# The order in which each engine takes the steps of its strands, written anew

## The reference

```python
x = x + 0.5 * _L0_ffn_ref(_layernorm(x), ...)    # squared ReLU with a sigmoid gate and a time shift
x = x + _L0_attn_ref(_layernorm(x), ...)         # gated linear recurrence, 32 states
x = x + 0.5 * _L0_ffn_ref(...)
x = x + 0.5 * _L1_ffn_ref(...)                   # top-1 router over 8 experts, capacity, one shared weight
x = x + _L1_attn_ref(_layernorm(x), ...)         # Mamba forward and backward, 256 channels x 16 states
x = x + 0.5 * _L1_ffn_ref(...)
x = x + 0.5 * _L2_ffn_ref(...)                   # 16 experts, two chosen, and a shared one
x = x + _L2_attn_ref(_layernorm(x), ...)         # causal attention, 16 heads of 8
x = x + 0.5 * _L2_ffn_ref(...)
x = x + 0.5 * _L3_ffn_ref(...)                   # 8 experts, two chosen
x = x + _L3_attn_ref(_layernorm(x), ...)         # attention with normed q and k, 16 heads of 8
x = x + 0.5 * _L3_ffn_ref(...)
```

## Time and profile before

| quantity | value |
|---|---|
| median of 3 runs | 2844.74 us (2841.48 to 2850.73) |
| profiled execution, its own time | 2852.38 us |
| its span, first to last instruction | 2850.6 us |
| mean granted clock of TensorE | 0.922 |
| PE, DVE, ACT, POOL busy | 2455.4, 2273.0, 1692.7, 1377.6 us |
| instructions in the span | 31759 |
| moved by DMA | 251.37 MB, mean 88 GB/s |

### The profile page before, as it was taken

One profiled execution on the slowest core, in us unless ns is written; L12 is line 12 of the kernel. 1 busy time (PEld: TensorE's weight loads), 2 busy tenths in 40 slices (PEclk: granted clock), 3 DMA queues, 4 the chain that ended last, 5 costly groups with the idle time before them and its releaser, 6 DMA issues. The chain is left out here.

```text
span 2850.6 us, 31759 instructions
## 1 busy us (share of the span) xinstructions
PE 2455.4 (86%) x8664; PEld 881.1 (31%) x8664; DVE 2273.0 (80%) x3833; ACT 1692.7 (59%) x2849; POOL 1377.6 (48%) x1295
## 2 busy tenths in 40 slices
...
GB/s 96 102 111 99 117 107 62 104 104 138 64 105 65 96 128 100 49 105 129 100 106 50 116 90 123 60 97 107 124 67 136 73 62 58 46 77 48 44 25 34
DMA packets 159395, 251.37 MB, mean 88 GB/s; under 512 B 20089, under 2 KB 58233, under 8 KB 158961
## 3 DMA queue, kind: packets, MB, share of 16 engines
...
## 5 line engine op out<-in xcount | busy, mean ns | idle before, releaser
L1411 DVE TENSOR_REDUCE nmx<-ps 128x1 f32<-128x512 f32 (+3 forms) x864 | 536.2, 662 | 80.2 <-PE ps L621 78.5
L1802 ACT ACTIVATE tN<-ps 128x512 f32<-128x512 f32 (+1 forms) x896 | 463.8, 565 | 156.5 <-PE ps L621 154.3
L621 PE MATMUL ps<-tN,strip 128*64 128x512 f32 (+3 forms) x2048 | 476.8, 556 | 0.8 <-DVE hN L1434 0.6
L1910 POOL TENSOR_TENSOR rb<-duf,bs 128x512 f32<-128x512 f32 x256 | 324.2, 1280 | 235.0 <-DVE ps L1473 127.1
L1910 POOL TENSOR_TENSOR rb<-dub,bs 128x512 f32<-128x512 f32 x256 | 323.2, 1274 | 162.4 <-DVE ps L1473 84.1
L1473 DVE TENSOR_TENSOR_SCAN ps<-ps,rb 128x512 f32<-128x512 f32 x304 | 365.4, 1218 | 30.5 <-ACT ps L1856 28.5
L621 PE MATMUL ps<-hF,W 128*128 128x512 f32 x592 | 345.1, 667 | 51.2 <-DVE tF L1328 25.3
L621 PE MATMUL ps<-Ks,Qs 128*128 128x512 bf16 (+3 forms) x1024 | 297.5, 358 | 68.2 <-DVE nmx L1411 57.9
L1919 POOL TENSOR_TENSOR rh<-rh,cs 128x512 f32<-128x512 f32 x208 | 265.4, 1287 | 170.3 <-DVE rh L1473 166.4
L621 PE MATMUL ps<-tF,W 128*128 128x512 f32 x528 | 288.4, 633 | 19.7 <-POOL tF L1936 16.2
L1929 POOL TENSOR_TENSOR tF<-tF,cr 128x512 f32<-128x512 f32 x128 | 163.9, 1282 | 270.4 <-DVE tF L1332 158.0
...
## 6 DMA issues: line engine op xcount, KB each, us to landing
cr<-shares SPq DMA_DIRECT2D x248, 256.0 KB, 3.5
bs<-rowsf SPq DMA_DIRECT2D x128, 256.0 KB, 3.7
cs<-rowsf SPq DMA_DIRECT2D x128, 256.0 KB, 3.4
bs<-rowsb SPq DMA_DIRECT2D x128, 256.0 KB, 3.7
cs<-rowsb SPq DMA_DIRECT2D x128, 256.0 KB, 3.4
...
```

The costliest lines, as they stand in the source:

```text
L621: return eng.matmul(o, l, r, start=start, stop=stop, skip_group_check=skip_group_check)
L1411: red(nmx[:, 4 * qt + 2 * (i // 4) + a, i % 4:i % 4 + k], o[:, 0:k * nk].rearrange("p (k c) -> p k c", k=k), AX.X, ALU.max, negate=True).t ...
L1802: act(tN[m % NP][:, a, 0:nq], PA[a][:, 0:nq], ACT.Exp).then_inc(s_ex, 1)
L1910: tt(rb[n % NBB][:, g, :], du[p][:, g, :], bs[n % NB][:, :], ALU.mult).then_inc(s_bp[g], 1)
```

## The change

Only the table `ORDER` is written anew, for all five engines. The diff holds nothing else. In the kernel's own terms the sequence in which each engine takes its strands is made anew with the array's spacings as traced; the strands, their steps, tiles and semaphore waits are those of before. The first and the last lines of each text (the diff's lines in between are of the same kind):

```diff
--- before.py
+++ after.py
     "sp": (
-        "M1S25M1S32M1S26M1S18F1S2F4S3F1S1F1S4F2S4M1S10P1S2P2S1P7S9M1S2X1S7F1S1F4S3F1S1F1S4F2S18F4S2F2S2F1S2F1S2F1S2M1S8P1S4"
...
-        "S5P4F9X1F8P1F1P5F1P4F9P1X1P1F8P4F5P2F2P1F1P1F2X1F1P1F3P1F5P4F1P4F9X1F9P10X1F2X1F9"
+        "M1S29M1S30M1S34M1S10F1S2F3S2F2S2F2S2F1S4M1S12P1S4P9S8M1X1S8F4S4F2S4F2S4F1S16F4S3F1S1F1S3F1S1F1S2F1S2M1S8P1S2P7F1P1"
...
+        "X1F7"
     ),
     "pe": (
-        "L22M1L1M1L1M2L3M1L1M2L2M1D1L2S1D1S1L1D1S1L2D1S1D1L1S1L1D1S1L1D1S1M1L1D1S1L1D1S1M1L1M1D1S1L1D1S1M1D1S1L1D1S1D1S1M1"
-        "D1S1D1S1M1D1S1M1D1S1L1D1S1D1S1M1L1M1D1S1L1D1M1S1D1S1D1M1S1D1L1D1M1L1M1D1S1D1L1S2M1L1D1S1L1D1S1M1D1S1D1L1S1D1L2M1S1"
...
-        "L1A2L1A2L1A2L3A16X2A2X2A2X2A2X2A2X2A2X2A2X2A2X2A1X14A1X2F1X3F1X6A1X2F1X1A1X1A1X2A2X2A2X2A2X2A2X2A2X2A2X2A2X2A2X2F1"
-        "X1A1X1A2X1A3F1A4F1A2F1A2F4A2F1A2F1A28F16"
+        "L22M1L1M1L1M2L3M1L1M2L2M1S1L1D1S1L1D1S2D1S1D2M1S1D1S1L1D1S1D1S1L1D1L1D1S1M1D1M1L1D1S1L1D1M1S1L1D1S2L1S1D1L1S1D1M1"
+        "L1M1D1L1S1M1D1L1S1D1S1L1D1S1M1L1M1D1S1L1D1M1S1D1S1D1M1S1D1L1S2L1M1D1M1L1D1S3D1M1L1S1D1L1S1D1S1D1L1M1D1S1L2D1S1M1S1"
...
+        "F1A6F1A1F2A3F3A2F1A1F1A1L1A2L1A3L1A2L1A2L1A1L1A2L1A2L1A2L1A2L2A14X2A2X2A2X2A2X2A2X2A2X2A2X2A2X2A2X2A1X11A1X2F1X1F1"
+        "X7A1X2A1X1A1X1F1X2A2X2A2X2A2X2A2X2A2X2A2X2A2X2A2X2F1X1A1X1A1X2A3X1A9F4A31F4A1F17"
     ),
     "dve": (
-        "L24M2L1M8L1M2L2D2S2D1S1D1L1S1L1D1L1S1L1D1S1M1D1S1D1S1M1D1S1D1L1S1D1S1D1S1M1D1S1D1S1M1L1D1S1D1S1M1D1M1S1M1D1S1L1M1"
-        "D1S1D1S1L2D1S1D1S1L2M1D1S1D1S1L1D1S1D1S1M1D1S1D1S1L3D1S1D1S1L2D1S1D1S1M1D2S2D1S1M1D1S1D1S1L1D1S1D1S1L1D1S1D1S1L1D1"
...
-        "X1F6X1F9L1F4L1A1F1X3A1X2A1X7F1X2F1X1F7X1F1X1F1X1F1X1F1X1F1X1F1X1F1X1F2X3F2X2F2X3F2X5F2X3F2X3F2X3F2X3F2X2F1X5F1X7F1"
-        "X2F1X1F1X1F4X1F16L3A1X28A1X2A1X13F1X2F2X2F3X2F4X2F3X2F3X2F3X2F3X13A1F1A2F39"
+        "L24M2L1M8L1M2L1S1L1S1D1S1D1S1M1D1S1D1S1M1L1S1D1S1D1M1S1D1S1D1L1D1S1D1S1M1D1S1D1S1L1D1S1D1S1M1D1S1D1S1L1D1S1D1M1S1"
+        "D1M1D1S1D1M1D1S1L1D1S1D1S1D1S1D1M1S1D1S1D1S1L1S1D1S1D1M1S1D1S1D1S2D2L1M1D1S1L2D1M1S1L1D1L1S1L2D1L1D1L1S1L1S1L1D1L1"
...
+        "A1F1X3A1X2A1X7F1X2F1X1F14X1F2X3F2X3F2X3F2X6F2X3F2X3F2X3F2X3F2X3F1X5F1X7F1X2F1X1F1X1F1X1F1X1F1X1F1X1F5X1F11L3A1X27"
+        "A1X2A1X14F1X2F1X2F4X2F5X2F3X2F3X2F4X2F1X13A3F40"
     ),
     "act": (
-        "L30M2L2M3L2M2L2M1L1M2L2M8L2D1L2S1M2L2D1S1M1L2D1S1D1S1L2D1S1L2D1S1L2D1S1M1L1D1S1M1L1D1S1L3M1D1S1M1D1S1M4D1S1L2M3D1"
...
-        "L1A1L1A1L1A2L1A1L1A1L1A1L2A1L2A1L1A2L1A1L1A32F3A4F1A16F1A48F5"
+        "L30M2L2M3L2M2L2M1L1M2L2M8L2S1D1L1M2L2S1L1M1D1S1L2S1D1S1D1M1S1D2S1M1D1S1D1S1D1S1D1L2S1M1D1L2D1S1M2D1S1M2L1M1L1D1S1"
...
+        "F1A14F1A48F5"
     ),
     "pool": (
-        "L1M1D1S1D1S2D2S1D1S1L1D1S1D1S1D1S1D1S1L1D1S1D1S1D1S1D1S1D1S1D1S1M1D1S1D1S1D1S1D1S1M1D1S1D1S1D1S1D1S1D1S1D1S1D1S1D2"
...
-        "C2F3M1F5A2F3A1F5A5F9A1F1A1F2A1F1A1F3A3F2A1F7A1F3A1F2A1F2A5F14A1F2A10F5A1F3A2"
+        "L1M1S1D1S2D1S1D2S1D1S1D1S1D1S1D1S1D1S1D1S1L1D1S1D1S1D2S1D1S1D1S1L1M1S2D1S1D3M1S1D1S1D1S1D1S1D1S1D1S1D1S1D1S2D1S1D1"
...
+        "A10F3A1F3A2F2"
     ),
```

More of the change, by code:

```diff
@@ L69 @@
[L69 to L72, removed]
@@ new lines @@
+        "F1L1F1L1F1L1F2L3F1M1F2M1F3M1F1M1F2M1F2M1F4M1F4M1F1M1F4M1F3L1F1L1F1L1F1L6M2F1M1F1X2M1X3M1X2F1X2F1X1F1X5F1X4F1X1F1X3"
+        "F1X4F1X3L1X2F1L1X3F1X2L1X4L1X3F1L1F1L1X1F1L1A1L1A1L1A3L1A2L1F1A1M1A3F1A2F1A2M1A2F1A2F1M1A2M1A3M1A1F2L1A2F2L1F2A2F1"
+        "L1A2L1F1A1L1F1A1F1A2F1A2F1L1A2F1A1L1A1F1A2F2A2L1A1F1A2F1L1F1X1L1X1F1X2F1X4A1F1X2L1X1F1X3F1X2L1X3F2L1X3F1X3L1F1X3L1"
+        "F1X3L1X3F1X2F1X3L1X3L1X6F1L1X1F2X1F1L1X3F2L1X2F1X4L1X4M1X1F2M1F1X1F2M1F1M1A1F2A2F1A2M1A2F2A2M1F1A2F1A2F1A2F1A2M1A2"
@@ new lines @@
+        "F1A2F1A2F1A2F1A2M1A2F1A2F1M1A2F1A1M1F1A6L1A3L1A6F1L1A2L1F1A1L1A3L1A2L1F1L1A2L1A1F1A1M1A2F1A1M1F4X2F1A1X1M1A1X2M1F1"
+        "X2M1F1X6F1X1L1X3L1X4L1X3L1X4L1X2L1F1L1X1F1X4L1X2L1X3L1X2L1X1F1M1F2X1F3M1X1F2A1F1A2F1M1A2F2A1M1A4F1A2M1A2F1A2F1A1F1"
+        "L1A3F2L1A5L1A1L1F1A2F2L1A1F1A2F2L1F1A2F2A1L1F1A3F2A3F1L1A1F1A2F1L1A1F1L1A2F1A2F2L1X2A1F2X2F1L1X2F1X1L1X2F2X2F1X3F1"
+        "X3L1X2F1L1X3F1X2L1X5F2X1L1X5L1X5L1X2F1X1L1X3F1X1F1L1X2F1X2L1X1F1X1F1X1M1X2F1X1M1X3F2X4F1M1F1M1X1F2M1F1A1F1A2M1F1A2"
@@ new lines @@
+        "F1A2F1A2F1A2M1A2F1A2F1A2F1A2F1A2M1A1F1A1F1A2M1A1F1A1F1A2F1A2M1A2F1L2F1A2L1A2L1A2L1A2L1A2L1A2L1A2L1A2F1A2M1A2F1A2M1"
+        "A4F1A1F1A3M1F1A1F3M1A1F2X1M1F1X2F1X2L1F1X2L1X5L1X4L1X4L1X2L1X2L1F1X3F1L1X3L1X3L1X2L1X2M1F2X1F1X4F1X1F1X1F1M1F2X1F2"
+        "M1A1F2M1A2F1A1M1A2F1A3F1L1A1F1A2L1A2F1A2F1L1A3L1A2L1A2F1A2F2L1F1A2F2L1F1A2F1A2L1F2A2L2F2A2F1A2L1F2A3F1A3F1A2L1F1A1"
+        "F1A2L1X1F1X1F1X1A1F1X1L1X2F1L1X3F2X3L1X1F1X1F1X1L1X2F1L1X3F1X9F1X3F1X2L1X6L1X2F1L1X2F1X1F1X1L1X2F1X2M1F1X2F1X3F1X3"
@@ new lines @@
+        "L1X3L1X1F1X2F1X3L1F1X1F1X1M1F1X2F1X1M1X1F1X2F1X2F1X2M1X1F1M1F1M1X1F3M1F2A1F2A2F1A2M1F2A2F1A2F1A2M1A2M1A2F1A2F1A2F1"
+        "A2M1A2F1A2F1A2L1A2F1A2L1A2F1L1A1L1A5L1A2L1A2L1A2L1A2L1A2F1A2F1A2M1A4M1A2F1A2F1A2F1A1X2F1X2F1X1F1A1X2F2M1X3F1X2F1X1"
+        "M1X3M1F1X11L1X3L1X5F1X3F1X2L1X4L2X1F2L1F1L1A1F1A2F1A2L1A2F1A4F1A2F1A2F1A2F1A2L1A2F2A2L1A2L1F1M1A3F1A3F1A4F1A2M1A4"
+        "F1A2F1A4M1A1X2M1X4A1X1F1X3F1X2F1X2F1X3F1X2F1X2F1X3F1X1F1X3F1X3F1X2F1X2F1X14F1X3F1X2F1X3M1X1F1X2F1X3F1X1F3X1F2M1F1"
@@ new lines @@
+        "A1F1M1A2F1A5F1A1F1M1A2F2A2L1A4L1A6F1A2F2A2F1A2F2A2L1F1A2L1F2L1F1A2F2A2L1F1A2L1F2A2F1A2L1A2F1A2F1A2F1A2L1A2F1A2F1A2"
+        "F1A2M1F2A2F2A3M1F1X2F2A1X2F1M1X3M1X4M1X4F1X2F1X10F1X1F1X1F1X5F1X2F1X1F1X4F1X1F1X2L1F1X1L1F1L1A1F1L1A2L1A1F1L1F1L1"
+        "A3L1A2L1A1F1A1F1L1F1L1A2F2A2F1A2F2A2F1A4F1A2F2A4F1A2F1A4F1A2F1A4F1A2F1A2F1A2F1A1X2F1X1F1X2F1A1X1F1X1F2X3F1X5F1X2F1"
+        "X3F2X2F1X3F2X2F1X3F2X2F1X3F3X1F1X2F1X2F1X3F1X3L1F1X2L1F1X5L1F1L1F1L1F1X3L1X3L1X1L1X1F1L1X3F3X1F3A1F1A10F1A2F1A2F3"
@@ new lines @@
+        "D1M1X7M1X2M1X1M1X10D1X7F1X5S1D1X2L1X7F1X3F1X1F1X1F1S1F1S1F1D1X1F1S1F2D1F1S1L1F1D1F1S1D1L1S1D1S1D1S1D1S1F1D1F1M1D1"
+        "M1S1M1D1S1M1D1S1D1S1M1F1M1S1M1D1F1S1M1F1S1F1S1F1S1F2D1F2D1F1D1F1D1F1S1F2M1F2S1F2D1S2F1M1A1D1S1F1D2F1D1S1F1L1S1F1D1"
+        "S3D1S1F1L1D1S1D1F1D1S2D1F1S1D1S1D2F1D1S1D1S3F1L2F1S1D3F1D1S3F1X2S1X1L1X3A1L1F1A1X2L1F1X2D1X1L1X5F1X3F1D1X3L1F1X3D1"
+        "S1X3D1S1X3F1X2F1X1F1L1F1X1F1X1F2X1F2X1F1X1F1X1F1X1F1X1F1X1F1X1F1X1F2X1L1X2F1D1X1L1S1L1D1L1F1L1D1X1F1X2L1X1L1F1L2X1"
@@ new lines @@
+        "D1F1M1F1D1S1D1M1S3D1S1D1S1F1M2F1M1F1D1F1S1F1M1F4S1F1D1F1X1F1X1F1X1F1X1F1A1F1X1F2A1X2F1X4F1X3F1X4F1X3F1X4F1X3F1X4F1"
+        "X14F1X3M1D1F1X5F1X6F1X3F1X1M1X1D1F1X1F1X1D1S2F1S1M1F1D1S1D2M1F1S5D1F1D1S1F4D1F2S1F2D1F1D1F1S1F1S1F2D1F1D1F1S1F2D1"
+        "S1F1L1D1S1F1D1S2F1D2S1D1F1S1D1F1D1S1D1S1D1S1F1A1F1D1S1D1F1D1S2F1S2F1S1D2F1S1D1S2D1F1D1S2F1D1S1D2F1D2S1D1F1D1S2F1D1"
+        "S1D1F1M1D1S1D1S1D1F1M1A1S1X1S1X1A1F1X2F11X1F1M1F1X1F1X1F2X1F1X1F1X1F1X1F1X1F1X1M1X1M1X1M1X27F1X5L1F22L2F3A1F32X3A1"
```

207 lines of the change are left out of this document (92 added, 115 removed).

## The result

The changed kernel takes 2779.2 us (median of 4 runs, 2772.23 to 2786.76) where the kernel before took 2843.11 beside it: a ratio of 0.9772, interval 0.9753 to 0.9791. 2852 was forecast, and the range began at 2810. The profiled execution took 2776.37 us, its span 2774.6.

A forecast was written before the change was run, and what follows sets the result against it. It took DVE, with PE close behind, to pace the first part and PE the tail; table loads +0.9, end of first part +3, drift +3 and zeros gave +7 on 2844.74, so 2852 us, own range 2838 to 2866.

The forecast's parts named there:

- Drift between two orders: Mid-run attentions: DVE reaches attention outputs up to 24 us later than PE wants them; bounds 0 to +24, taken +3.
- Short gaps: PE steps needing DVE or ACT results: gaps for maxima +5 us, ACT's -6; taken 0, bounds -6 and +17.
- slower rival: DVE holds PE at the attentions, the drift is not absorbed and work moves into the tail: 2873 us, chance 0.26.
- The end of the first part: Work leaves for the tail: tail +29 us, first part -22 or -31; net +7 or -2, taken +3.
- The faster rival: Stalls thin out in the first part, PE's 330 us idle sheds 33: 2812 us, chance 0.30.
- three signs that the forecast named as its refutation: Tail hardly grows; hN or nmx waits grow over 17 us; PE's first-part idle falls by tens of us.
- 159 table loads: On ACT, loads rise from 151 to 159, 10.3 us of ACT work mostly hidden: +0.9 us, bounds 0 and +10.3.
- At the start: Around 93 to 141 us PE is sparser, hidden by a full DVE: 0; uncovered it would be 8 us.
- SyncE's later stores: Stores of B and C rows stand nearer their first readers: taken 0, bounds 0 to +3.3 us at each of four places.

The follow-up runs named there:

- the old interleaving: Order of before up to 2245 us, changed kernel's order for the rest: 0.9967 to the kernel before; the reverse splice, with the old tail: 0.9853.
- the three pairs: Old and new order with PE's work cut (2811.7, 2760.47 us), as it is (2843.11, 2779.2) and with score and up products doubled (2997.88, 2913.3).
- the one split of strands: Scan strands S, D, C placed as in the new order, all else as in the old: 1.0918 to the kernel before; the reverse: 1.0768.
- my planners: Orders planned with PE too fast or as traced, against the kernel before: list schedule 1.0162, 1.0282; search from old order 0.9962, 1.0108; from new 0.9961, 1.007.

## Why the prediction was wrong

- **The first and the deciding failure is the step "Drift between two orders", with "Short gaps" beside it: the sum has no term for what VectorE waits for.** The drift step found that DVE's steps on the array's results come later in DVE's own work than PE's do, and priced this as harm to PE, 0 to +24 us, of which I took +3, and a slower rival at 2873. PE was not held up: its waits for hN are 9.0 us after 9.7, for nmx 55.7 after 57.9. The price had to be asked of the other side. DVE paces the first part, so what counts is what DVE waits for, and there its waits for PE fell by 31 us and its idle time by 51. The prediction called DVE the pace and then costed the order by PE's waits. That the drift itself is what spared DVE the 31 us is not shown: shifting DVE's steps later by a rule spared it 22 and cost 4.6% of the time.
- **"Short gaps" had the same fault.** It counted PE's own work between a product and its dependent product, and ACT's gaps behind the scores, and took 0; the waits of DVE for ACT, -22 us, are in none of its counts.
- **"The end of the first part" was right in kind and mis-sized.** 33 DVE instructions were to leave at a reduction's price, 20 us; 33 left, of which 28 are reductions, with 20.2 us. The first part was to lose 22 us: in the old interleaving it lost 16, in the new 38. The tail was to grow by 29: it grew by 8 (old first part) to 12 (new), and between the two kernels by 5, 13 and 14 in the three pairs. The moved matmuls cost PE 12.9 us there (516.76 to 529.64), half of the 26 that I took from whole-span means. Net -8 to -26 where +3 was forecast.
- **The faster rival was right in mechanism and too timid.** It took a tenth of PE's idle, 33 us, and 2812. DVE's idle time fell by 50.9 of 220, almost a quarter, and its busy time by 30: 20.2 us are the moved reductions, 4.8 are less blocking by GpSimd, the rest other steps. Two of the three signs that the forecast named as its refutation came: the tail hardly grew, and PE's idle in the first part fell by tens of us, 330.4 (2212 - 1881.65) to 307.7.
- **Right:** 159 table loads, at 1283 ns each. The trace has no drain behind them, as the earlier trace rows had it: in 133 of the 159 the next activation starts within 0.1 us.

```profile
L1543 ACT ACT_TABLE_LOAD x159 | 204.0, 1283 | 3.5 <-PEq L2149 0.7
```

  Ten us more of ACT's work seem to hide as they were to (DVE waits less for ACT than before), though no run has the loads alone. At the start PE is sparser from 93 to 141 us as forecast (34.73 us of work where it had 36.94) and DVE denser (47.71 after 45.81), at a granted clock of 0.93 both times. The first batch ends 14 us later and the second 11 us earlier, and the first 690 us together are worth 0.25%, interval 0.02 to 0.47. SyncE's later stores cost little: in the first part DVE's waits for a DMA are 5.4 us after 1.6, and POOL's 186.2 after 211.0.

What is settled: the gain lies on VectorE in the first part, as 30 us of busy time, 20 of them reductions moved past its end, and 51 us of idle time, a part of it waits for the array that grow with the array's load. Moving the work is worth 0.3 to 0.8% of the time. What stays open is which feature of the interleaving brings the 1.5% that remain when the moved work is put back. It is not uniform lateness, not one side of the one split of strands that was tried, and with my planners a better cost of the array did not bring it. With all the work kept, none of the other orders, made by splice, rule or search, is faster than the changed one; that would suit a fit of the whole that no single feature names, but does not show one. Swapping the order on single engines alone was not tried.
